# Handing the first batch over between two fused attention stages, and summing the experts on TensorE

## The reference, cut to what matters

```python
x = x + diff_attention(layernorm(x))        # L0_attn: 16 heads, two softmaxes, rms-normalised q and k
x = x + L0_ffn(layernorm(x))                # grouped attention, then a mixture of experts
x = x + L1_attn(layernorm(x))               # 8 blocks of linear attention and a feed-forward
x = x + L1_ffn(layernorm(x))                # ternary feed-forward

def L0_ffn(h0):
    residual = h0
    h = rmsnorm(h0, ln1_w)
    q, k, v = rope(h @ Wq), rope(h @ Wk), h @ Wv       # 16 query heads, 4 key/value heads
    h = clip(residual + softmax_causal(q k / sqrt(8)) v @ Wo, -100, 100)
    hn = rmsnorm(h, ln2_w)
    topv, topi = top_k(softmax(hn @ Wr), 2);  topv = topv / sum(topv)
    moe = sum of the two chosen experts' silu(hn @ Wg) * (hn @ Wu) @ Wd, weighted by topv
    return clip(h + moe, -100, 100)
```

## Time and profile before

| | us |
|---|---|
| median of 3 runs | 3329.98 |
| lowest and highest | 3326.60, 3334.91 |
| the profiled execution, own time | 3320.53 |
| its span, first to last instruction | 3318.8 |
| PE busy | 2971.5 (90%) |
| DVE busy | 2598.0 (78%) |
| ACT busy | 2294.1 (69%) |
| POOL busy | 2071.2 (62%) |
| mean granted TensorE clock | 0.940 of full |

### The profile page before, as it was taken

One profiled execution on the slowest core, in us unless ns is written; L12 is line 12 of the kernel. 1 busy time (PEld: TensorE's weight loads), 2 busy tenths in 40 slices (PEclk: granted clock), 3 DMA queues, 4 the chain that ended last, 5 costly groups with the idle time before them and its releaser, 6 DMA issues. The chain is left out here.

```text
span 3318.8 us, 65954 instructions
## 1 busy us (share of the span) xinstructions
PE 2971.5 (90%) x22194; PEld 1843.6 (56%) x22194; DVE 2598.0 (78%) x7048; ACT 2294.1 (69%) x3519; POOL 2071.2 (62%) x2319
## 2 busy tenths in 40 slices
PE   5999996799898988499259999999999999999979
PEld 2555553344444444388236666666666666666658
DVE  4666663887887875376569999999999999999967
ACT  4877773365665657254468888888888888888833
POOL 3444443234555453377658888888878888888744
PEclk8999997698999999699669999999999999999979
DMA  4445443222222220486310000000000000000001
GB/s 105 114 102 119 114 101 88 61 57 67 52 58 68 65 67 21 100 284 187 99 45 1 16 1 7 11 6 11 1 16 1 16 1 16 1 16 1 1 14 39
DMA packets 178767, 178.12 MB, mean 54 GB/s; under 512 B 18660, under 2 KB 159167, under 8 KB 178334
## 3 DMA queue, kind: packets, MB, share of 16 engines
q1 hardware_dynamic: 169342, 157.03, 19.0%
q0 software_dynamic: 9088, 16.88, 1.5%
HBM read 99.74 MB, written 75.86 MB: 53 GB/s over the span
## 5 line engine op out<-in xcount | busy, mean ns | idle before, releaser
L2703 PE MATMUL lb_FF<-lb_h,lb_w 128*128 128x512 f32 x1024 | 480.7, 591 | 0.0
L2815 ACT ACTIVATE lb_h<-lb_H,lb_prm 128x512 f32<-128x512 f32 x512 | 337.4, 685 | 45.9 <-PE lb_H L2694 43.6
L2939 DVE TENSOR_SCALAR lb_z<-lb_M,lb_mv,lb_rstd 128x128 f32<-128x128 f32 x1024 | 344.9, 399 | 4.0 <-POOL lb_rstd L2852 3.4
L2852 POOL TENSOR_TENSOR lb_rstd<-lb_rstd,half 128x4 f32<-128x4 f32 x256 | 261.2, 1020 | 36.6 <-issue 0.4
L2703 PEld LDWEIGHTS lb_FF<-lb_h,lb_w 128*128 128x128 f32 x1024 | 193.2, 189 | 145.6 <-issue 92.0
L1538 POOL TENSOR_SCALAR_AFFINE_SELECT da_PT<-da_PT 128x1024 f32<-128x1024 f32 x128 | 145.9, 1145 | 197.7 <-ACT da_PT L1468 197.7
L2688 PE MATMUL lb_H<-lb_x1s,lb_w 128*128 128x512 f32 x512 | 264.3, 516 | 5.4 <-issue 5.4
L2931 DVE BATCH_NORM_STATS2 lb_stats<-lb_M 128x6 f32<-128x128 f32 x1024 | 225.2, 280 | 23.2 <-PE lb_M L2647 14.6
L559 ACT ACTIVATE ga_PT<-ga_S 128x384 f32<-128x384 f32 x256 | 111.7, 489 | 178.5 <-PE ga_S L375 178.5
L1473 ACT ACTIVATE da_PT<-da_SY 128x1536 f32<-128x1536 f32 x128 | 185.2, 1447 | 70.6 <-PE da_SY L1343 69.4
L2886 POOL TENSOR_TENSOR lb_y<-lb_ao,XC 128x512 f32<-128x512 f32 x128 | 192.9, 1507 | 38.3 <-ACT lb_ao L2802 38.1
(11 more groups left out here) (365 smaller groups left out, 8815.9 us busy)
## 6 DMA issues: line engine op xcount, KB each, us to landing
moe_w<-experts_dram SPq DMA_DIRECT2D x39, 384.0 KB, 3.4
da_qT<-da_stq SPq DMA_DIRECT2D x64, 192.0 KB, 4.4
da_kT<-da_stk SPq DMA_DIRECT2D x64, 192.0 KB, 5.5
ga_qT<-ga_stq SPq DMA_DIRECT2D x32, 384.0 KB, 5.9
moe_x<-moe_xs SPq DMA_DIRECT2D x39, 258.0 KB, 4.0
tc_g<-moe_ys SPq DMA_DIRECT2D x32, 256.0 KB, 3.3
lb_split<-moe_parts SPq DMA_DIRECT2D x8, 896.0 KB, 6.0
da_stq<-da_parts SPq DMA_DIRECT2D x16, 384.0 KB, 2.4
```

What stands on the lines that cost most here:

```text
L2703: pe.matmul(FF[:, :], w2[:, k, :], h[:, k, :], start=(k == 0), stop=(k == KC - 1)).then_inc(ff_filled, 1)
L2815: act.activation(h[:, k, :], H[:, k % 2, :], ACT.Gelu_apprx_tanh, bias=col(FB1 + k, i)).then_inc(h_ready, 1)
L2852: pool.tensor_tensor(out[:, :], out[:, :], C["half"][:, 0:NT], ALU.pow).then_inc(done, 1)
L2939: last = v.tensor_scalar(z[:, t, :], M[:, t * P:(t + 1) * P], mv[:, t, 0:1], rstd[:, t:t + 1], ALU.subtract, ALU.mult)
```

## The change

1. The prelude's block goes; its transfers and casts move into diff_attention's programs, and each constant has a semaphore of its own. The first transpose waits for `ident` alone.
2. In diff_attention batch 0's k, turned k, sums and v go to the banks of the scores (`lead`), which are still unused, so these products no longer wait for one another's readers. Batch 1's `project_k` and `project_qs` move behind the first scores.
3. Grouped attention's batch 0 is prepared inside diff_attention: measured, normalised, turned and projected at m = 1 to 7 of b = 14 and split at m = 0 to 4 of b = 15, in the places where a 17th batch would stand. SP stores and loads its q and k there. The G tiles live through both stages.
4. grouped_attention's loop runs from b = -1. Ahead of it stand the scans of pairs 0 to 3, with batch 1's steps between them.
5. The weight of each token's expert is made per batch (`ratios` on ACT, `weigh_rows` on POOL) and travels in a new column 129 of the row; `take` multiplies by it. `make_shares` and its wait go.
6. In `collect` PE adds both experts' rows and `H` by three products with the identity (accumulated in PSUM, full 128x512 float32), and DVE clips out of PSUM. The scaling on POOL and ACT goes.

```diff
-ROW = P + 1
+ROW = P + 2
 # grouped_attention, PE
-            for b in range(-3, NB + 2):
+            scan(0)
+            scan(1)
+            turn_x(1)
+            scan(2)
+            project_q(1)
+            scan(3)
+            project_qs(1)
+            project_kk(1)
+            for b in range(-1, NB + 2):
...
-                if b == -2:
-                    for m in range(AHEAD - 7):
-                        for part in range(3):
-                            max_scores(m, part)
 # grouped_attention, ACT
+            def ratios(r):
+                act.wait_ge(gap_ready, r + 1)
+                if r >= 2:
+                    act.wait_ge(scattered[r % 2], 16 * 2 * NT * (r // 2))
+                act.activation(ratio[:, r % 2, :], gap[:, r % 2, :], ACT.Exp).then_inc(ratio_ready, 1)
...
+                    if s == 2 and exists(r):
+                        ratios(r)
 # grouped_attention, POOL
+            def weigh_rows(r):
+                pool.wait_ge(ratio_ready, r + 1)
+                pool.tensor_scalar(weight[:, :], ratio[:, r % 2, :], 1.0, None, ALU.add)
+                pool.drain()
+                pool.wait_ge(row_ready, r + 1)
+                pool.tensor_tensor(rows[:, r % 2, :, P + 1], weight[:, :], minus_one[:, :], ALU.pow
+                                   ).then_inc(weighted, 1)
...
+                    pool.tensor_tensor(rows[:, r % 2, :, P + 1], rows[:, r % 2, :, P + 1],
+                                       ratio[:, r % 2, :], ALU.mult)
...
+            scales(1)
+            pool.memset(v12[:, :, :, :, :], 0.0)
...
+            first_residual()
+            residual(1)
+            for b in range(-1, NB + 2):
...
+                    if s == 4 and exists(r):
+                        weigh_rows(r)
 # grouped_attention, DVE
+            measure(1)
+            v.memset(bm[:, :, :], BIG)
+            v.drain()
+            scan(0)
+            scan(1)
+            centre(1)
+            scan(2)
+            cosines(1)
+            scan(3)
+            sines(1)
+            rotate_k(1)
+            v.wait_ge(w_loaded, 16 * 5)
...
+            v.tensor_copy(matsb[:, :, :], mats[:, :, :])
 # diff_attention
+        def lead(c, use):
+            if c:
+                return M[:, (0, 0, 1, 1, 0)[use], :]
+            return (SX[:, 0, :], SX[:, 1, :], SY[:, 0, :], SY[:, 1, :], SY[:, 2, :])[use]
...
+            def g_project_q():
+                pe.wait_ge(xT_copied, NB + 1)
+                pe.wait_ge(g_scaled, 1)
+                pe.matmul(M[:, 0, :], G["wq"][:, 0, :], xnT[:, :], start=True, stop=True
+                          ).then_inc(filled[Q], 1)
...
             project_q(1)
-            project_k(1)
-            project_qs(1)
             pe.wait_ge(zeroed, 1)
             score_diagonal(0)
             score_later(0)
+            project_k(1)
+            project_qs(1)
...
+                    if m == 2 and c == NB:
+                        g_sum_k()
+                    if m == 6 and c2 == NB:
+                        g_project_q()
+                    if m == 7 and c2 == NB:
+                        g_project_kk()
+                    if m == 3 and c == NB:
+                        g_project_v()
-                    if m == 5 and next_but_one:
+                    if m == 5 and c2 <= NB:
                         turn_x(c2)
+                    if m == 7 and c2 == NB:
+                        g_project_qs()
 # diff_attention, POOL
+                    if m == 1 and c2 == NB:
+                        g_scales()
 # diff_attention, SP, at its end
+            sp.wait_ge(g_ones_loaded, 32)
+            sp.wait_ge(g_landed, 64)
 # expert_tiles, DVE
-                v.tensor_copy(y[:, j % YR, :], D[:, j % 2, :]).then_inc(y_ready, 1)
+                v.tensor_tensor(y[:, j % YR, :].rearrange("p (t d) -> p t d", t=NT),
+                                D[:, j % 2, :].rearrange("p (t d) -> p t d", t=NT),
+                                weight[:, j % YR, :].unsqueeze(2).to_broadcast([P, NT, P]), ALU.mult
...
+                v.tensor_copy(weight[:, j % YR, :], x[:, j % XR, :, P + 1])
 # collect
+            def add_experts(b):
+                pe.wait_ge(loaded[b % GR], 32 * (b // GR + 1))
+                if b >= 3:
+                    pe.wait_ge(clipped, b - 2)
+                for j in range(2):
+                    pe.matmul(A[:, b % 3, :], C["ident"][:, :],
+                              g[:, b % GR, j, :, :].rearrange("p t d -> p (t d)"),
+                              start=(j == 0), stop=False)
+                pe.matmul(A[:, b % 3, :], C["ident"][:, :],
+                          H[:, NT * b:NT * b + NT, :].rearrange("p t d -> p (t d)"),
+                          start=False, stop=True).then_inc(summed, 1)
...
+            add_experts(0)
+            add_experts(1)
+            for b in range(NB):
+                if b + 2 < NB:
+                    add_experts(b + 2)
+                turn_x(b)
...
+                v.wait_ge(summed, b + 1)
+                v.tensor_scalar(acc[:, :, :].rearrange("p t d -> p (t d)"), A[:, b % 3, :], 100.0, -100.0,
+                                ALU.min, ALU.max).then_inc(clipped, 1)
```

More of the change, by code:

```diff
@@ L357, in score @@
                     pe.wait_ge(m_loaded, 32 * (n // 8 + 1))
+                if n == 8 and part == 0:
+                    pe.wait_ge(ones_loaded, 32)
                 max_before = u + 3 * AHEAD - 2
@@ L413, in weigh, with scan @@
                 return last
-            pe.wait_ge(w_scaled, 1)
-            pe.wait_ge(zeroed, 1)
-            pe.wait_ge(ones_loaded, 32)
-            for b in range(-3, NB + 2):
+            def scan(m):
+                for part in range(3):
+                    max_scores(m, part)
+            scan(0)
[7 more added lines that the diff above has]
+            for b in range(-1, NB + 2):
                 p, c, c2, c3, r = b - 1, b + 1, b + 2, b + 3, b - 2
@@ L691, in scatter @@
                         ).then_inc(scattered[r % 2], 16)
-            scales(0)
-            residual(0)
             scales(1)
-            for b in range(-3, NB + 2):
+            pool.memset(v12[:, :, :, :, :], 0.0)
+            pool.memset(blank[:, 0:P], 0.0)
+            pool.memset(blank[:, P:P + 1], 2.0 * NTOK)
+            pool.memset(blank[:, P + 1:ROW], 0.0)
+            pool.memset(minus_one[:, :], -1.0)
+            pool.drain()
+            pool.memset(v12[:, :, :, :, VD:VD + 1], 1.0).then_inc(zeroed, 1)
+            first_residual()
+            residual(1)
+            for b in range(-1, NB + 2):
                 p, c2, c3, r = b - 1, b + 2, b + 3, b - 2
@@ L1644, in add_out @@
                                 ).then_inc(out_done, 1)
+            v.memset(C["half"][:, :], -0.5)
+            v.memset(C["ln_eps"][:, :], LN_EPS)
+            v.memset(C["rms_eps"][:, :], 2.0 ** -23)
+            measure(0)
+            centre(0)
             v.memset(V[:, :, :, :, :], 0.0)
```

601 lines of the change are left out of this document (371 added, 230 removed).

## The result

The changed kernel takes 3278.56 us (median of 5 runs, 3274.55 to 3291.15) against 3330.71 for the kernel before (5 runs in the same group, 3326.60 to 3334.91): ratio 0.9854, 95% interval 0.9832 to 0.9877, or 52 us less. I had forecast 3299.5, 31 us less. Three more groups of runs with the two kernels gave 0.9845 (0.9827 to 0.9863), 0.9897 (0.9876 to 0.9917) and 0.9848 (0.9832 to 0.9865).

The account below looks back on a forecast made before the run. It took start waits, PE in the last full pass, DVE's late scans in the grouped head, and DVE, ACT and POOL in the collection as limits; terms sum to -30.5 us, 3330.0 to 3299.5, range 3286 to 3318 (about 8 in 10).

Parts of the forecast that it names:

- start: Start of differential attention: earlier x transfer and separate banks bring first scores sooner, -6 us, bounds -10 and -3.
- last passes of the first stage: Differential attention's last two passes: preparing grouped attention's batch 0 there costs PE time in b = 15, +4.3 us.
- head: Head of grouped attention: batch 0's round and most of batch 1's wait go, -28.5 us, bounds -31 and -24.
- steady: Steady grouped attention: POOL's extra product per batch delays `rotate`, +1 us, bounds 0 and +3.5.
- tail: End of grouped attention: `weigh_rows(15)` adds to POOL's queue, +0.5 us, bounds 0 and 1.6.
- experts: Experts' stage, bound by POOL: the second column read adds one cast ahead of the first result, +0.2 us.
- collection: Collection: PE becomes the bound at 3.8 us a batch against 4.03, -2 us, bounds -5 and +4.
- A: Collection (`add_experts`): PE stays at 1.2 GHz, net +23 us, time 3353; chance 6%.
- B: Head of grouped attention: interleaved batch 1 steps stall DVE, half the gain goes, net -17 us, 3313; chance 11%.
- C: Differential attention's passes: POOL's small operations and DVE's splits cost 7 us more, net -23, 3307; chance 7%.
- D: Experts' stage: each added DVE cast holds up POOL through the shared port, 6.6 us, net -24, 3306; chance 5%.
- E: Hand-over to grouped attention: batch 0's q and k land late, so scans start late, a few us; chance 1%.

Follow-up runs that it names:

- again_before: The kernel before, run again unaltered and profiled: median 3329.85 us.
- again_after: The changed kernel, run again unaltered and profiled: median 3276.03 us.
- experiment 2: Changed kernel with batch 0's first products back in two shared banks: 3288.40 us; first score at 34.5, 2 us later.
- experiment 6: Clock time lost against steady-stage length over profiles, five of them giving the 0.84 line; reordered splits of q and k against the changed kernel (3280.57): 3286.45 and 3292.95 us.
- c_dve: Changed kernel with the experts' rows summed by two DVE additions instead of PE products, no scaling: first to last clip 60.8 us against 51.1.
- c_two: Changed kernel with two PE products in the sum, DVE adding H: 3340.20 us on a long-experts occasion; clips 52.0 against 51.1.
- experiment 3: Changed kernel with batch 1's steps behind the four first scans: 3287.54 us; pair 4's scan at 24.9 us instead of 20.0 to 21.1.
- experiment 5: Changed kernel without per-batch weights, in a group on an occasion with experts at 254 to 257 us (kernel before: 3380.12): 3343.34 us.
- g_noweigh: Changed kernel without the per-batch expert weights, column 129 holding 0.5: 3343.34 us on a long-experts occasion.
- b_pesum: Kernel before with the collection's sum on PE but the scalings kept: first to last clip 57.0 us against 62.0 before.

## Why the prediction was right in most parts and wrong in its sum

From the pair `again_before` and `again_after`, whose own times (3328.03 and 3275.70) lie near the medians. *Hand-over* is from the last yT copy of differential attention to grouped attention's first DVE instruction, *tail* from the last yT copy of the steady stage to the first result scatter:

```
                                   predicted   measured
start                                -6          -9.6    first yT copy 96.9 -> 87.3
last passes of the first stage       +4.3        +3.5    445.2 -> 448.7
hand-over                             0          -0.3
head                                -28.5       -30.5    51.4 -> 20.9
pair 4 to the first yT copy           0          -0.7
steady                               +1          -2.3    653.7 -> 651.4
tail                                 +0.5        -4.0    61.5 -> 57.5
experts                              +0.2        -1.2
collection                           -2          -8.9    last scatter to last clip, 76.1 -> 67.2
blocks and ternary stage              0          +1.7
sum                                 -30.5       -52.3
```

- **Collection, the step that failed.** "Three 128x512 products ... 3.8 a batch ... against 4.03": a batch takes 3.40 in the mean, and it took (1686.0 - 1623.8) / 15 = 4.15 by the clips. The mechanism held in part. PE is at full clock and is the bound of the last eight batches, but of the first ones, summed ahead, DVE is, at 3.0; I had PE's pace for all. PE's pace was mis-sized too: I charged each product 1.05 and the transposes behind them in full; in the trace the first two products take 1.88, the third 1.02, the transposes 0.66, and partly overlapped they fit into 3.48 (mean of the last eight). And I took 4.03 from ACT's rows where DVE's clips give 4.15. Fifteen times 0.75 is 11.2; the first clip comes 2.0 later relative to the last scatter. The stage gained 8.9, where my bound was -5.
- **Start.** Normalised x at 7.8 (7.5 forecast) and the last third at 24.8 (25.5 to 27.5) were right. Wrong was the trip through DRAM, put at 11.6: it takes 7.6. Before, the last load was issued at 40.9 and the score waited until 46.2 behind PE's two products. I had that as the bound (-10) and should have taken it. Of the 10 us, about 7.4 are the earlier transposes and, by the first score, some 2 the banks (experiment 2).
- **Last passes.** +4.3 forecast; 29.36 against 24.98 in the trace, +3.5 to +4.4 for the stage in every pair. The cover and its price were read correctly.
- **Head.** The waits came where they were put: 2.2 ahead of scan 2 (2.3 forecast), 1.2 to 2.1 for `project_kk` (2.0). Pair 4 stood 20.0 to 21.1 us after the hand-over, 23.2 forecast; the waits ahead of cosines and scan 3 did not occur. PE was at full clock for part of this stretch (0.63 in the mean of 540 to 580, 0.50 assumed), which may be why; no run tests it. The bound of -31 held.
- **Steady, tail, experts.** What the weights cost is not shown: 0 to 3 us on the occasions with short experts (experiment 6), inside my bounds. The -2.3 of the table is this pair's; the two other profiles give +7.0 and +10.7. The tail was 58.5 and 61.5 in the two profiles before and 57.1 to 59.6 in eight after on the same three occasions: its -4.0 is mostly one execution's.
- **The range.** Start, head and collection all left the forecast on the same side, -3.6, -2.0 and -6.9. These three alone would have put the sum at 43 us and the time at 3287, still just inside the range (3286); the steady stage and the tail, where the execution decides, took it out. My low end of 3287 already had every bound on the low side (-10 + 3.4 - 31 + 0 + 0 + 0.2 - 5 = -42.4), so it was not their adding up that failed: in this pair the collection passed its own bound by 3.9, the tail by 4.0 and the steady stage by 2.3, and the experts lay 1.4 below their term.
- **Rivals.** A: the clock is full in the collection; with the sum on DVE, `c_dve`, it is 0.50 again. The Trainium skill (TensorE: Matmul & The Clock Gate, What's actually happening) has activity release the half rate, and here the trace agrees: half rate until 1585.0 and full from there to 1639.6 in `again_after`. In `c_two` it fell twice between. B: the interleaving gains (experiment 3). C: the passes paid no more. D: experts 204.5 and 205.5 before, 204.3 to 205.0 after (203.2 to 206.0 with the variants), with 39 more reads of a column; rival D's 6.6 is not there. The Trainium skill's rule on it (SBUF — State Buffer, Who interferes with whom) shows in no row here. E: the first scan came 1.7 us after the hand-over.

Open: why the gain was 52 to 54 and 48 us on three occasions and 39 on a fourth, with long experts. On the two occasions with long experts the steady stage with the weights took 661 to 671 us at 33 to 43 us of clock lost, 11 to 15 more than the line of experiment 6 gives (651.4 at 35.7, 0.84 us for each us lost). In the group of experiment 5 it was 11 more with them in both (`c_two`, 661.3 at 34.1; `c_dve`, 665.6 at 39.0), 4 without (`g_noweigh`, 664.4 at 45.9) and 3.5 in the old grouped stage (`b_pesum`, 657.4 at 38.7). That the weights cost some 7 us there, though at most 3 on the other occasions, would fit; a profile or two of each do not settle it, and no run was made for it.

## What to carry to other kernels

Where a term is a rate times many batches, read the rate of the engine that bounds the stage and overlap PE's small work with its products before multiplying; here 0.4 us too much a batch, over fifteen, was more than the whole term. A stage prepared alone is worth moving into the idle of the stage ahead: here the moved work cost 4 us in the last full pass and saved 31 at the head. Between two executions of one kernel compare stages, and sum a clock loss over the stage's own stretch: a window fixed in time cuts two kernels at different steps. Removing one of two loads that hold a stage together says little: dropping the scalings gave 1.2 us, moving the sum 5.0, both 10.9.

## What the runs showed of the hardware that was not expected

- In the steady stage, where PE is 88% busy, the granted clock still falls to half once in nearly every batch (some 46 us), and with the same waits to 0.01 us it stays there for 7 us in one execution and 14 in another. The steady stage moves with it, from 651 to 664 us with one code on occasions with the same experts' stage, and is most of what the profiled executions of one kernel differ by (9 of 13 us between `after` and `again_after`); the runs of the changed kernel lie between 3272 and 3292. PE was busy 2.44 of the 5 us in the stretch in which the clock fell, with waits of 1.3 and 1.7 us.
- The experts' stage took 203 to 206 us on three occasions and 254 to 266 on two others, for every kernel that ran there, and of the other stages in the table of the experiments all but the steady one repeated. PE's weight loads waited at "issue" for 31.3 us between 1380 and 1580, in 13 waits of up to 4.9 us, in `c_two` (first line), against 0.6 us in `again_after` (second; group, us in total, times, longest). In the seven other profiles with long experts it was 23 to 38 us. What they waited for the profile does not show.

```profile
PEld moe_GU L2148 <- issue: 31.3, 13, 4.9
```
```profile
PEld moe_GU L2148 <- issue: 0.6, 1, 0.6
```
